# First layer of a two-layer message-passing kernel: one-hot products in float32 instead of three bf16 parts

## The reference

```python
x_j = node_features[col]
m = jnp.einsum('ei,ej,ijh->eh', x_j, edge_attr_e3nn, W_msg_tp) * norm_msg_tp
m = jax.nn.silu(m)
m = m @ W_msg_lin * norm_lin
agg = jax.ops.segment_sum(m, row, num_segments=n_nodes)
u = jnp.einsum('ni,nh,ihk->nk', node_features, agg, W_upd_tp) * norm_upd_tp
u = jax.nn.silu(u)
u = u @ W_upd_lin * norm_lin
return node_features + u
```

## Time and profile before

| | |
|---|---|
| median of three runs | 5498.1 us |
| profiled execution, span from first to last instruction | 6222.7 us |
| first layer's edge loop in the profile | about 219 to 2934 us |
| second layer's edge loop in the profile | about 3040 to 6070 us |
| busy shares of the span: PE, DVE, ACT, POOL | 74%, 75%, 49%, 65% |
| granted TensorE clock, mean | 0.844 |

### The profile page before, as it was taken

The page is one execution under the profiler, slowest core; times in us unless marked ns, Lnnn a source line. Parts: engine busy times, 40 slices in busy tenths (PEclk is TensorE's granted clock), DMA queues, the critical chain, the costliest instruction groups (busy, mean ns, idle before and its releaser), DMA issues. The chain is left out here.

```text
span 6222.7 us, 73121 instructions
## 1 busy us (share of the span) xinstructions
PE 4615.3 (74%) x17323; PEld 2099.6 (34%) x17471; DVE 4690.8 (75%) x7634; ACT 3048.5 (49%) x7980; POOL 4041.5 (65%) x3679
## 2 busy tenths in 40 slices
PE   2377677776777777778588888888888888888881
PEld 1133333333333333334233333333333333333330
DVE  5566665666666665666588988988999889899996
ACT  1122222222122221221377777877877777787883
POOL 5765666666666666664477777777777777777754
PEclk5677787787777877878699999999999999999995
DMA  4222222222222222221122222222222222222224
GB/s 131 67 60 59 61 62 59 62 63 60 60 61 60 61 61 60 62 61 45 25 75 76 76 76 76 77 75 75 81 78 76 76 76 76 76 76 76 76 70 115
DMA packets 350921, 435.22 MB, mean 70 GB/s; under 512 B 172480, under 2 KB 252747, under 8 KB 350509
## 3 DMA queue, kind: packets, MB, share of 16 engines
q0 software_dynamic: 128160, 187.16, 13.0%
q1 hardware_dynamic: 222605, 246.69, 12.7%
HBM read 214.10 MB, written 219.29 MB: 70 GB/s over the span
## 5 line engine op out<-in xcount | busy, mean ns | idle before, releaser
L1082 POOL DMA_INDIRECT xg<-x1tab,edge x1712 | 1962.0, 1146 | 775.7 <-issue 567.6
L628 POOL DMA_INDIRECT bg<-btab,mt x1568 | 1699.3, 1084 | 1017.6 <-DMA e<-in_edge_attr_dram 552.8
L830 PE MATMUL pagg<-ohh,stt 128*128 128x512 bf16 x4557 | 1761.4, 420 | 381.0 <-issue 357.0
L1172 PE MATMUL ps<-work,ident 128*128 128x512 f32 x3424 | 1754.3, 648 | 224.2 <-ACT ps L1116 90.1
L831 PE MATMUL pagg<-ohh,stt 128*128 128x270 bf16 x4704 | 1421.1, 302 | 364.3 <-issue 346.5
L1235 DVE TENSOR_TENSOR work<-pw,xg 128x1024 f32<-128x1024 f32 x856 | 910.6, 1086 | 297.0 <-PE pw L1166 154.8
L787 ACT CAST joined<-rest 128x256 bf16<-128x256 f32 x196 | 79.7, 407 | 2113.0 <-DVE rest L713 1501.7
L1172 PEld LDWEIGHTS ps<-work,ident 128*128 128x128 f32 x3424 | 668.6, 206 | 970.5 <-issue 852.4
L830 PEld LDWEIGHTS pagg<-ohh,stt 128*128 128x128 bf16 x4704 | 486.0, 103 | 1124.3 <-issue 661.1
L740 DVE TENSOR_TENSOR res<-sact,s 128x128 f32<-128x128 f32 x196 | 56.6, 289 | 980.9 <-remote 870.9
L1141 ACT ACTIVATE work<-work,mt 128x256 f32<-128x256 f32 x1712 | 734.5, 498 | 89.6 <-DVE work L1235 65.6
(11 more groups left out here) (269 smaller groups left out, 4189.7 us busy)
## 6 DMA issues: line engine op xcount, KB each, us to landing
ssum<-state SPq DMA_DIRECT2D x214, 512.0 KB
smax<-state SPq DMA_DIRECT2D x214, 256.0 KB
etab<-joined SPq DMA_DIRECT2D x389, 102.0 KB
xg<-x1tab,edge POOLq DMA_INDIRECT x1712
bg<-btab,mt POOLq DMA_INDIRECT x1568
e<-in_edge_attr_dram SPq DMA_DIRECT2D x392, 32.0 KB
e<-in_edge_attr_dram SPq DMA_DIRECT2D x392, 16.0 KB
btab<-bst SPq DMA_DIRECT2D x7, 512.0 KB
```

What stands on the lines that cost most here:

```text
L628: g.indirect_dma_start(bg[:, h, i, :], None, btab, bass.IndirectOffsetOnAxis(ap=mt[:, h, 0, i:i + 1], axis=0)).then_inc(gathered[h], 16)
L830: pe.matmul(pagg[:, 0, :], w, ohh[:, h, i, 0:CUT], start=False, stop=False, skip_group_check=True)
L1082: g.indirect_dma_start(xg[:, b % 4, i, :], None, x1tab, bass.IndirectOffsetOnAxis(ap=edge[:, b, i, EW - 1:EW], axis=0)).then_inc(x_in[b % ...
L1172: return pe.matmul(ps[:, i // G4, :], ident[:, :], work[:, b % 4, i, :, :, :].rearrange("p i a o -> p (i a o)"), start=False, stop=i % G4 ...
```

## The change

`ohl`, `stt`, `ohh`, `iota_hi` and the zero operand `zb` become float32. `s1`, `s2`, `s3`, `res`, `ohx` and the instructions that make them go away. `stt` is made from `sact` and `ohl` directly, in two products of four edge slots each (128x512) in place of three of eight slots. PE issues two float32 matmuls for each edge slot, 16 a block. DVE's wait for the silu moves from the start of `stationaries` to the first product.

```diff
-        iota_hi = sb("iota_hi", [128, HI], F16)
+        iota_hi = sb("iota_hi", [128, HI])
...
-            ohl = tsb("ohl", [LANES, 2, J, LO], BF16)
-            stt = tsb("stt", [LANES, 2, 3, J, LO, D], BF16)
-            ohh = tsb("ohh", [LANES, 2, J, HI], BF16)
-            zb = tsb("zb", [LANES, CUT], BF16)
+            ohl = tsb("ohl", [LANES, 2, J, LO])
+            stt = tsb("stt", [LANES, 2, J, LO, D])
+            ohh = tsb("ohh", [LANES, 2, J, HI])
+            zb = tsb("zb", [LANES, CUT])
...
                     v.wait_ge(used, k + 1)
-                    v.wait_ge(act_done, 2 * k + 2)
-                    v.tensor_tensor(res[:, h, :, :], sact[:, h, :, :], s1[:, h, :, :], ALU.subtract).then_inc(res_done, 1)
                     rest_of(k, c)
                     for i in range(J):
                         v.tensor_scalar(ohh[:, h, i, :], iota_hi[0:LANES, :], hilo[:, h, 0, i:i + 1], None,
                                         ALU.is_equal).then_inc(ohh_done, 1)
-                        if i == 0:
-                            v.wait_ge(res_done, k + 1)
-                            v.tensor_copy(s2[:, h, :, :], res[:, h, :, :]).then_inc(s2_done, 1)
                         if i == 2:
-                            v.wait_ge(s2_done, k + 1)
-                            v.tensor_tensor(s3[:, h, :, :], res[:, h, :, :], s2[:, h, :, :], ALU.subtract).then_inc(s3_done, 1)
                             lowest_of(k, c)
-                        if i == 1:
-                            v.wait_ge(ohx_done, k + 1)
-                        if i in (3, 4, 5):
-                            part = (s1, s2, s3)[i - 3]
-                            if i == 5:
-                                v.wait_ge(s3_done, k + 1)
-                            v.tensor_tensor(stt[:, h, i - 3, :, :, :],
-                                            part[:, h, :, :].unsqueeze(2).to_broadcast([LANES, J, LO, D]),
-                                            ohx[:, h, :, :, :],
+                        if i in (3, 5):
+                            if i == 3:
+                                v.wait_ge(ohl_done, k + 1)
+                                v.wait_ge(act_done, k + 1)
+                            w = slice((i - 3) // 2 * H4, ((i - 3) // 2 + 1) * H4)
+                            v.tensor_tensor(stt[:, h, w, :, :],
+                                            sact[:, h, w, :].unsqueeze(2).to_broadcast([LANES, H4, LO, D]),
+                                            ohl[:, h, w, :].unsqueeze(3).to_broadcast([LANES, H4, LO, D]),
                                             ALU.mult).then_inc(stt_done, 1)
...
-                    act.wait_ge(ohl_done, k + 1)
-                    act.copy(ohx[:, h, :, :, :], ohl[:, h, :, :].unsqueeze(3).to_broadcast([LANES, J, LO, D])).then_inc(ohx_done, 1)
                     act.wait_ge(msg_done, k + 1)
                     act.activation(sact[:, h, :, :], msg[:, h, :, :], ACT.Silu, scale=float((D * DE) ** -0.5)).then_inc(act_done, 1)
-                    act.activation(s1[:, h, :, :], msg[:, h, :, :], ACT.Silu, scale=float((D * DE) ** -0.5)).then_inc(act_done, 1)
...
-                        pe.wait_ge(stt_done, 3 * k + 3)
+                        pe.wait_ge(stt_done, 2 * k + 2)
                         pe.wait_ge(ohh_done, J * k + J)
                         for i in range(J):
-                            for a in range(3):
-                                w = stt[:, h, a, i, :, :].rearrange("p l c -> p (l c)")
-                                pe.matmul(pagg[:, 0, :], w, ohh[:, h, i, 0:CUT], start=False, stop=False, skip_group_check=True)
...
+                            w = stt[:, h, i, :, :].rearrange("p l c -> p (l c)")
+                            pe.matmul(pagg[:, 0, :], w, ohh[:, h, i, 0:CUT], start=False, stop=False, skip_group_check=True)
```

More of the change, by code:

```diff
@@ L488, in gnn @@
             sact = tsb("sact", [LANES, 2, J, D])
[L489 to L492, removed]
-            ohl = tsb("ohl", [LANES, 2, J, LO], BF16)
-            stt = tsb("stt", [LANES, 2, 3, J, LO, D], BF16)
-            ohh = tsb("ohh", [LANES, 2, J, HI], BF16)
-            zb = tsb("zb", [LANES, CUT], BF16)
+            ohl = tsb("ohl", [LANES, 2, J, LO])
+            stt = tsb("stt", [LANES, 2, J, LO, D])
+            ohh = tsb("ohh", [LANES, 2, J, HI])
+            zb = tsb("zb", [LANES, CUT])
             fixed = tsb("fixed", [1, 2, 3 * C])
-            ohx = tsb("ohx", [LANES, 2, J, LO, D], BF16)
             pagg = st.enter_context(nc.psum_tensor("pagg", [128, 2, CUT], F32))
@@ L514, in gnn @@
             act_done = sem("l0_act_done")
-            res_done = sem("l0_res_done")
-            s2_done = sem("l0_s2_done")
-            s3_done = sem("l0_s3_done")
             ohl_done = sem("l0_ohl_done")
-            ohx_done = sem("l0_ohx_done")
             rows_made = sem("rows_made")
@@ L527, in gnn @@
             block = st.enter_context(nc.Block())
+            H4 = J // 2
             def split(h, lo, hi):
@@ L824, in _ @@
                         k, h = B4 * t + c, c % 2
-                        pe.wait_ge(stt_done, 3 * k + 3)
+                        pe.wait_ge(stt_done, 2 * k + 2)
                         pe.wait_ge(ohh_done, J * k + J)
                         for i in range(J):
-                            for a in range(3):
-                                w = stt[:, h, a, i, :, :].rearrange("p l c -> p (l c)")
-                                pe.matmul(pagg[:, 0, :], w, ohh[:, h, i, 0:CUT], start=False, stop=False, skip_group_check=True)
-                                ins = pe.matmul(pagg[:, 1, 0:HI - CUT], w, ohh[:, h, i, CUT:HI], start=False, stop=False,
-                                                skip_group_check=True)
+                            w = stt[:, h, i, :, :].rearrange("p l c -> p (l c)")
+                            pe.matmul(pagg[:, 0, :], w, ohh[:, h, i, 0:CUT], start=False, stop=False, skip_group_check=True)
+                            ins = pe.matmul(pagg[:, 1, 0:HI - CUT], w, ohh[:, h, i, CUT:HI], start=False, stop=False,
+                                            skip_group_check=True)
                         ins.then_inc(used, 1)
```

## The result

The changed kernel takes 5422.0 us (median of four runs, 5416.4 to 5426.3) against 5498.0 us before in the same job: ratio 0.9862, interval 0.985 to 0.9874. It is **1.4% faster**, 76 us. Forecast were 5532 us, a range of 5430 to 5645 and "slower" as the likeliest. Both the direction and the range missed; the first rival, 5444 us, was nearest.

A forecast was written before the change was run, and what follows sets the result against it. The prediction took POOL's gathers, about 11 us a block, to bound the kernel. Its +0.15 us a block over 196 blocks (29 us) and 5 us at the ends, on 5498 us, gave 5532 us, range 5430 to 5645 us.

The forecast's parts named there:

- the first rival: Fewer products free POOL: 0.2 to 0.3 us a block saved on gathers, 5444 us, chance 0.28.
- What bounds before: First layer's edge loop: POOL's gathers bound the timed run at 11.1 us a block; the profile's extra 724.6 us is PE's stutter.
- TensorE: PE's matmuls: three bf16 passes become four, 8.0 to 10.5 us a block, hidden beside POOL's 11.1 us.
- DVE: DVE's stream: small instructions and a product go, longer `ohh` rows come; 8.67 to 9.1 us a block, hidden behind POOL.
- POOL: The gathers beside DVE's new stream: longer rows +0.35, fewer products -0.2, together +0.15 us a block, 29 us in all.
- The product's -0.2: POOL's gathers: one of three products gone, so they are held 0.2 us a block less.
- The +0.35 for longer rows: POOL's gathers: 3.2 a block fall beside longer float32 `ohh` rows, each held some 0.1 us more, +0.35 us a block.
- The ends: Last block's uncovered matmuls, +2.5 us, and first matmuls at half clock, a few us: together 5 us.
- The page's rule: Ports shared by DVE and POOL: whole-instruction exclusion would cost more than taken, the second rival's time, 5655 us, chance 0.10.
- Fewer products free POOL: POOL's gathers: float32 rows hold no more than bf16 ones, 0.2 to 0.3 us a block saved, 5444 us, chance 0.28.
- PE becomes the bound: PE's matmuls at a mean clock of 0.9: 11.7 us a block, +0.6 us, 5620 us, chance 0.07.
- The span: Profiled execution: falls by a hundred us or more, with 32 matmul records a block in place of 48.

The follow-up runs named there:

- e0: The kernel before, unchanged, profiled once more: 6220 us, where before took a median of 6212 us in the same job.
- e4: The kernel before, unchanged, profiled again: 6083 us, with before at 6068 us in the job.
- e11: The kernel before, unchanged, profiled again: 6204 us, with before at 6229 us in the job.
- e14: The changed kernel with PE leaving out the matmuls of two of eight edge slots, job without stutter: 5412.6 us against 5498.8 for before.
- e7: Before without DVE's third product, PE using the first product twice, job with stutter: 6071 us against 6068.
- e15: Before with two bf16 parts, 32 matmuls a block, two products, no `s3`, PE's loop of two blocks, job without stutter: 5492.4 us against 5498.8.
- e6: Before with DVE's `ohh` rows written as float32 into their own buffer, PE reading rows of zeros, job with stutter: 6072 us against 6068.
- e12: The kernel before, unchanged, profiled in a job without stutter: 5505 us, with before at 5500 us in the job.
- e8: The changed kernel, unchanged, in a job with stutter: 6168.5 us against 6228.9 for before, ratio 0.9906.
- e1: Before with seven of the eight gathers of a block, job with stutter: 5928 us against 6212, ratio 0.9524.
- e13: Before with seven of the eight gathers of a block, job without stutter: 5243.6 us against 5499.6, ratio 0.9543.
- e3: Before with PE leaving out the third part's matmuls, 32 in place of 48 a block, job with stutter: 6085 us, ratio 0.9796.
- e9: Before with PE's hardware loop holding two blocks instead of four, job with stutter: 6218.6 us, ratio 1.0001.
- e10: Before with two bf16 parts, 32 matmuls a block, two products, no `s3`, PE's loop of two blocks, job with stutter: 5982 us against 6229.

## Why the prediction was wrong, point by point

- **What bounds before.** Right, though by a wrong road: POOL at 11.1 us a block was forecast, 11.08 from the gathers and 11.05 in the blocks were measured. The missing 725 us were put down to the profiler; in the jobs of e0, e4 and e11 the timed runs of before are as long (6068 to 6229 us), so they belong, as far as is known, to the job in which that trace was taken.
- **TensorE.** Right: 16 float32 matmuls in 10.5 us a block at full clock, the weight loads hidden. "That cover is thin, 0.6 us" was the sentence to follow up: POOL fell under it and PE became the bound, though e14 shows that POOL stands right behind: taking a quarter of PE's work away gave only 9 us more.
- **DVE.** Size right, a little low: 624 ns a row forecast, 658 measured (they are themselves held at times), the product 697 for 680, the block 9.6 us (10.5 less 0.87 of waiting) for 9.1. Hidden, as said.
- **POOL.** The step that failed: "I take +0.35 - 0.2 = +0.15 us a block". Measured were 8 x (1.080 - 1.012) = -0.54 us by the gathers, -0.49 us by the blocks. The product's -0.2 was the size found in e7, but e15, without stutter, has only 8 x (1.074 - 1.080) = -0.05. The +0.35 for longer rows has the wrong sign: e6 has -0.46 for the rows alone (in a job with stutter). The term was made by counting how much DVE time of each kind lies beside POOL and multiplying by a mean delay. But a gather is not held in proportion to time: it is held by the DVE instruction that is under way at its start, or by a product that follows at once, until that one's end, so what counts is how the steps of the two engines fit. The shares were also read from a stuttering trace, 0.5 us beside L724 and 0.5 beside the products; without stutter they are 0.13 and 0.64 (the table above). The timeline had it: three products in 2.5 us and a gather 0.06 us ahead of one of them.
- **The ends.** 5 us forecast; the tail grew by 10.
- **The page's rule.** The Trainium skill ("SBUF — State Buffer", on the shared ports) says that a DVE operation in a two-port mode and a GpSimd instruction exclude each other for the whole instruction. The prediction took the short delays as evidence against it. They are not. A row under way holds the gather to its end, as the row of e14 shown above, in agreement with the rule; a row that begins after the gather leaves it nearly alone, as in e12:

  ```profile
  1111.11 0.97 POOL L628 DMA_INDIRECT bg<-btab,mt  x1 [0.30 <-issue]
  1111.18 0.42 DVE L743 TENSOR_SCALAR ohh<-iota_hi,hilo 128x782 bf16<-128x782 f16 x1
  ```

  The price that the prediction worked out for it, each of 3.2 gathers a block held by half a row, did not come true: in the changed kernel rows hold gathers by 0.08 us a block, in e14 by 0.35. The longest delays in the rows shown stand beside operations with two inputs (1.56 and 1.32 us).
- **The rivals.** "Fewer products free POOL" named the right sign and nearly the right size, 5444 us, by luck: its reason, that a product, `res` and `s3` less free POOL, is refuted by e15, where a product and `s3` less give 6 us. "PE becomes the bound" came true without its price, since the clock stayed at 1.00.
- **The span.** It fell far more than "a hundred us", from 6222.7 to 5424.6, and not for the reason given (fewer matmul records): the two profiles are, as far as is known, of jobs of different sorts. Within one job with stutter the change gave 60 us (e8).

## What to carry to other kernels

Where POOL issues gathers beside a busy DVE, look at the two timelines side by side for the gathers that are longer than the shortest, and move the long DVE operations that stand in front of them, here the two-input products, apart before changing how much work there is: here an order of the same instructions was worth 139 us, and taking a whole product away in the wrong place 6 us. Before a difference between a profile's span and the timed median is called the profiler's, a second profile is worth its run. And when a hidden engine's new length comes within a few per cent of the bound, forecast what happens if the bound gets shorter.

## What was not expected of the hardware

- A gather of 128 rows lasts 0.94 us alone, and when held it is finished about 0.82 us after the end of the DVE instruction that held it: a bf16 product in e12 (1102.74 + 1.56 against 1103.48), the float32 multiplication L717 in the changed kernel, a float32 row in e14 (1107.90 + 1.30 against 1108.39). A product that begins 0.06 us after the gather still gets ahead of it (e12, 1102.80, with a row under way); a row that begins 0.07 us after it does not (e12, 1111.18).
- Two conditions of the same kernel on the same chip, 5496 and 6212 us, the slower one with matmuls a microsecond or more apart for some 20 us at a time (from 1645 us in the trace ahead of the prediction) and a granted clock of 0.50 from 1650 to 1665 us. A gather less is worth 284 us in the slower one (e1) and 256 in the other (e13), a third of the matmuls less 127 us in the slower one (e3); DVE's work (e6, e7) and the length of PE's loop (e9) move nothing there, yet a third of the matmuls, a product and `s3` less together give 247 us (e10), twice e3. Its cause was not found.
